# Layer two's attention sums on GpSimd and in one set of products, its steps at two places, and layer one's reciprocal last

## What is computed

```
# layer one, for each batch: softmax over the 256 keys m, then the values
attn = softmax(einsum('bnd,bdm->bnm', q, k), axis=2)
x = einsum('bcm,bnm->bcn', v, attn) + x
# layer two: 16 heads of 16, keys from the context (128, masked) and from x itself (128)
q = latents @ q_w + q_b
kv = concatenate([context, latents]) @ kv_w + kv_b
attn = softmax(where(mask, einsum(q, k) / 16, -inf))
attn_out = einsum('bhkn,bnhd->bkhd', attn, v)
attn_out = attn_out @ out_w + out_b + residual
out = gelu(rmsnorm(attn_out) @ w1 + b1) @ w2 + b2 + residual
```

## Time and profile before

| | us |
|---|---|
| runs | 2052.34, 2045.2, 2050.21 |
| median | 2050.21 |
| the profiled execution | 2044.37 |
| its span | 2042.6 |
| PE busy in it | 1849.2 (91%) |
| DVE, ACT, POOL busy | 1151.9, 973.4, 771.2 |
| mean granted clock of PE | 0.979 |
| layer one, from the start to about | 79 |
| layer two's loop, to about | 350 |

### The profile page before, as it was taken

How to read it: one execution, slowest core, us unless ns; L and a number is a source line. 1 busy time by engine, 2 the same in 40 slices (tenths; PEclk the granted TensorE clock), 3 DMA queues, 4 the chain that set the end, 5 groups by cost and what they waited for, 6 DMA issues and landing times.

```text
span 2042.6 us, 38530 instructions
## 1 busy us (share of the span) xinstructions
PE 1849.2 (91%) x15569; PEld 1566.9 (77%) x15569; DVE 1151.9 (56%) x2106; ACT 973.4 (48%) x2551; POOL 771.2 (38%) x819
## 2 busy tenths in 40 slices
PE   6788887898999999999999999999998788888798
PEld 4566665787888888888888888888877666666587
DVE  3444555445555555566665555556544677776743
ACT  4344444333444444444444444444444576675733
POOL 3322232402433435254353433425231476675500
PEclk9999999999999999999999999999999899998999
DMA  3000001101322223132231322222120000000000
GB/s 113 11 7 2 7 2 43 50 1 16 70 45 58 58 47 65 34 67 43 42 63 37 68 46 54 57 48 53 38 90 1 12 2 2 7 2 6 2 21 21
DMA packets 163201, 71.98 MB, mean 35 GB/s; under 512 B 136512, under 2 KB 154576, under 8 KB 163024
## 3 DMA queue, kind: packets, MB, share of 16 engines
q1 hardware_dynamic: 150672, 50.64, 12.6%
q10 hardware_dynamic: 12352, 18.88, 3.0%
HBM read 33.84 MB, written 2.10 MB: 18 GB/s over the span
## 4 chain that ended last, share of the span: by engine, by line
PE 75%; DVE 10%; ACT 9%; issue 3%; POOL 2%; DMA 1%; SPq 0%; ACTq 0%; DVEq 0%; POOLq 0%
PE ps_high L197 40%; PE ps_four L197 8%; PE ps_four L2667 5%; PE ps_four L2655 5%; PE ps_high L2552 2%; PE ps_high L2591 2%; ACT l_pt L1738 2%; PE ps_high L2446 1%; ACT l_sm L1783 1%; DVE l_sm L2173 1%; DVE l_sm L2183 1%; PE ps_four L2462 1%; ACT l_prob L1829 1%; PE ps_four L2467 1%; PE ps_high L2602 1%
## 5 line engine op out<-in xcount | busy, mean ns | idle before, releaser
L1839 ACT ACTIVATE l_ao<-ps_four,columns 128x512 fp32r<-128x512 f32 x128 | 88.0, 687 | 388.2 <-PE ps_four L2667 377.6
L1626 POOL TENSOR_TENSOR l_prob<-l_prob,l_mx 128x516 f32<-128x516 f32 x128 | 134.2, 1049 | 310.1 <-DVE l_mx L2214 310.1
L1829 ACT ACTIVATE l_prob<-ps_four,l_mx 128x129 f32<-128x129 f32 x512 | 181.8, 368 | 123.0 <-DVE l_mx L2207 122.8
L197 PE MATMUL ps_high<-l_hT,l_wq 128*128 128x512 f32 x768 | 210.8, 410 | 2.1 <-DVE l_hT L2096 2.1
L197 PEld LDWEIGHTS ps_high<-l_wo,l_ao 128*128 128x128 f32 x1536 | 198.0, 190 | 10.6 <-issue 0.7
L197 PE MATMUL ps_high<-l_wo,l_ao 128*128 128x256 f32 x1536 | 202.7, 281 | 0.0
L197 PE MATMUL ps_high<-l_wv,ctxT 128*128 128x512 f32 x768 | 200.3, 396 | 1.4 <-ACT l_qT L1810 1.4
L197 PE MATMUL ps_high<-ctxT,l_wk 128*128 128x512 f32 x768 | 198.5, 394 | 0.0
L1592 POOL TENSOR_TENSOR l_sm<-l_sm,l_mask 128x1024 f32<-128x1024 f32 x64 | 158.8, 2504 | 38.0 <-DVE l_sm L2173 38.0
L2220 DVE COPY l_planes<-l_prob 128x1024 uint16<-128x1024 uint16 x128 | 88.8, 694 | 149.0 <-POOL l_prob L1626 149.0
L197 PEld LDWEIGHTS ps_high<-ctxT,l_wk 128*128 128x128 f32 x768 | 144.8, 189 | 33.7 <-DVE l_V L2195 0.4
(11 more groups left out here) (295 smaller groups left out, 3791.5 us busy)
## 6 DMA issues: line engine op xcount, KB each, us to landing
l_staging<-in_L_xattn_wv ACTq DMA_DIRECT2D x8, 512.0 KB, 4.2
...
l_planesT<-l_planes SPq DMA_TRANSPOSE x128, 3.1
```

The costliest lines, as they stand in the source:

```text
L197: ins = e.matmul(out, a, b, start=start and i == 0, stop=stop and i == 2, skip_group_check=not check)
L1626: e.tensor_tensor(pr[:, :, 0:S + 1], pr[:, :, 0:S + 1], mx[:, 3, :].unsqueeze(2).to_broadcast([P, GB, S + 1]), ALU.mult).then_inc(sem("poo ...
L1829: ins = e.activation(pr.t[:, b, 0:S + 1], banks[b // 2].t[:, (b % 2) * (S + 2):(b % 2) * (S + 2) + S + 1], ACT.Exp, bias=mx[:, 1, b:b + 1] ...
L1839: e.activation(ao.t[:, 0, :], bk.t, ACT.Identity, bias=self.cols(f"L2_xattn_bv{at + 1}")[:, hd:hd + 1]).then_inc(sem("act.l2_values"), 1)
```

## The change

- **One set of sum products.** POOL adds the exponentials of the second half into the first one's tile (new stage `l1_fold`, 128x2048, in place). It waits until PE has read that tile in `over_v(n, 0)` and until the second half's exponentials are there. The 8 sum products then stand once in a batch, in a stage `l1_sums` of their own, which waits for the fold; `l1_ao` stands behind it.
- **Places.** `l1_over(n-1, s)` stand where they stood. `sums(n-1)` stands behind the shift and the first of two new `fill_pe`, directly ahead of `probs(n, 0)`. The credit is now given once a step (L1_STEPS). `fill` gives at most one advance, at two places; `fill_pe`, at two places, gives one or two and stops early at a stage with PE products. The `fill` ahead of `maxima(n, 1)` is gone.
- **Layer one.** The reciprocal and the product with it become a stage `l0_norm`, emitted last in a step.

```diff
-L1_RATE, L1_SLACK = (0.85, 1.0, 1.0, 1.0), 1
+L1_STEPS, L1_SLACK = (3.6, 4.25, 4.25, 4.25), 1
...
-            pl.free("mx", b, by=("pool.l0_scores", b))
+
+        def normalise(b):
+            pl.emit("l0_norm", b)
+            pl.free("mx", b, by=("pool.l0_norm", b))
...
-            for off, f in ((0, project), (1, softmax), (3, out), (2, values)):
+            for off, f in ((0, project), (1, softmax), (3, out), (2, values), (1, normalise)):
...
             if s == 1:
-                pl.slot(rec, "rec", n)
...
+                pl.emit("l1_fold", n)
+
+        def sums(n):
+            g, b = n // GB, n % GB
+            pl.slot(rec, "rec", n)
+            if b == 0:
+                pl.slot(ao, "ao", ("l1", g))
+            pl.emit("l1_sums", n)
+            pl.emit("l1_ao", n)
...
-            while ("l1_over", g * GB + GB - 1, 1) not in pl.place:
+            while ("l1_sums", g * GB + GB - 1) not in pl.place:
...
-        def fill(n, share=1.0):
+        def fill():
             nonlocal due
-            due += share * L1_RATE[min(n, B - 1) // GB]
-            while due >= 0.999:
+            if due >= 1.0:
                 due -= 1.0
                 next(rest, None)
+
+        def fill_pe():
+
+            nonlocal due
+            for _ in range(2):
+                at = len(pl.order)
+                due -= 1.0
+                next(rest, None)
+                if due < 0.0 or any(stage in ("l1_xT", "cols", "rows2", "out32", "norm_tr") for stage, _ in pl.order[at:]):
+                    return
...
         for n in range(B + 1):
+            due += L1_STEPS[min(n, B - 1) // GB]
...
-            fill(n, 0.25)
             if n < B:
                 maxima(n, 1)
...
-            fill(n)
+            fill()
             if n > 0:
                 over_v(n - 1, 1)
-            fill(n)
+            fill()
             if n < B:
                 run(shifted(n))
...
-            fill(n)
+            fill_pe()
+            if n > 0:
+                sums(n - 1)
             if n < B:
                 probs(n, 0)
             self.evac = "dve"
-            fill(n)
+            fill_pe()
             self.evac = "act"
...
+        def l1_fold(n):
+
+            pt = [use["pt", n, s].t for s in range(2)]
+            q.wait_ge(sem("pe.l1_over"), n + 1)
+            q.wait_ge(*pl.event(("empty", "four", n, "prob", 1)))
+            e.tensor_tensor(pt[0][:], pt[0][:], pt[1][:], ALU.add).then_inc(sem("pool.l1_fold"), 1)
...
+        def l1_sums(n):
+            pt, bk = use["pt", n, 0].t, use["over", n]
+            q.wait_ge(sem("pool.const:o"), 3)
+            q.wait_ge(*pl.done("pool.l1_fold", n))
```

More of the change, by code:

```diff
@@ L623, in over_v @@
         def over_v(n, s):
-            g, b = n // GB, n % GB
             if s == 0:
                 pl.bank(over, "over", n)
-            pl.emit("l1_over", n, s, v_done=ready[g])
+            pl.emit("l1_over", n, s, v_done=ready[n // GB])
             if s == 1:
-                pl.slot(rec, "rec", n)
-                if b == 0:
-                    pl.slot(ao, "ao", ("l1", g))
-                pl.emit("l1_ao", n)
-                pl.free("over", n)
-                pl.free("rec", n, by=("pool.l1_ao", n))
-                for s in range(2):
-                    pl.free("pt", n, s, by=("full", "over", n))
-                    if b == GB - 1:
-                        pl.free("vv", ("l1", g), s, by=("full", "over", n))
+                pl.emit("l1_fold", n)
[6 more added lines that the diff above has]
+            pl.emit("l1_ao", n)
+            pl.free("over", n)
+            pl.free("rec", n, by=("pool.l1_ao", n))
+            for s in range(2):
+                pl.free("pt", n, s, by=("full", "over", n))
+                if b == GB - 1:
+                    pl.free("vv", ("l1", g), s, by=("full", "over", n))
         def end(g):
@@ L1494, in l1_heads, with l0_norm @@
             ins.then_inc(sem("pool.l1_heads"), 1)
-        def l0_scores(b):
+        def l0_norm(b):
             pr, mx = use["prob", b].t, use["mx", b].t
-            q.wait_ge(*pl.done("dve.l0_scores:r", b))
+            q.wait_ge(*pl.done("dve.l0_norm", b))
             e.tensor_tensor(pr[:], pr[:], mx[:, 2, :].unsqueeze(2).to_broadcast([P, 2, D]), ALU.mult).then_inc(
-                sem("pool.l0_scores"), 1)
+                sem("pool.l0_norm"), 1)
         def w_pool(name, c0):
@@ L1963, in l0_scores, with l0_norm @@
                 sem("dve.l0_scores:m"), 1)
+        def l0_norm(b):
+            mx = use["mx", b]
             q.wait_ge(*pl.event(("empty", "l0_scores", b)))
-            e.reciprocal(mx.t[:, 2, :], mx.t[:, 1, :]).then_inc(sem("dve.l0_scores:r"), 1)
+            e.reciprocal(mx.t[:, 2, :], mx.t[:, 1, :]).then_inc(sem("dve.l0_norm"), 1)
         def l0_values(b):
@@ L2294, in vector_program @@
         stages = dict(const=const, l2_bws=l2_bws, l2_pbs=l2_pbs, l1_const=l1_const, rows2=rows2, l1_max=l1_max, l1_shift=l1_shift,
-                      out32=out32, norm_tr=norm_tr, cols=cols, l0_loads=l0_loads, l0_project=l0_project, l0_scores=l0_scores, l0_values=l0_values, l0_out=l0_out, w_dve=w_dve,
+                      out32=out32, norm_tr=norm_tr, cols=cols, l0_loads=l0_loads, l0_project=l0_project, l0_scores=l0_scores, l0_norm=l0_norm, l0_values=l0_values, l0_out=l0_out, w_dve=w_dve,
                       l1_xT=l1_xT, l1_key_mask=l1_key_mask, norm_stats=norm_stats, norm_var=norm_var,
@@ L2371, in l0_values @@
             pr = use["prob", b].t
-            q.wait_ge(*pl.done("pool.l0_scores", b))
+            q.wait_ge(*pl.done("pool.l0_norm", b))
             bk = fill("l0_tr", b)
@@ L2456, in l1_over @@
             q.wait_ge(*pl.event(("empty", "four", n, "prob", s)))
-            q.wait_ge(sem("pool.const:o"), 3)
             bk = fill("over", n) if s == 0 else use["over", n]
@@ L2461, in l1_over @@
                     for r in range(4):
-                        e.matmul(bk.t[32 * r:32 * r + 32, S * j:S * j + S], vv[:, b, i, j * P + 32 * r:j * P + 32 * r + 32],
-                                 pt[:, r, (2 * j + i) * S:(2 * j + i + 1) * S], start=(j, i, s) == (0, 0, 0),
-                                 stop=i == 1 and s == 1, tile_position=(0, 32 * r), skip_group_check=True)
+                        ins = e.matmul(bk.t[32 * r:32 * r + 32, S * j:S * j + S], vv[:, b, i, j * P + 32 * r:j * P + 32 * r + 32],
+                                       pt[:, r, (2 * j + i) * S:(2 * j + i + 1) * S], start=(j, i, s) == (0, 0, 0),
+                                       stop=i == 1 and s == 1, tile_position=(0, 32 * r), skip_group_check=True)
+            if s == 0:
+                ins.then_inc(sem("pe.l1_over"), 1)
+        def l1_sums(n):
+            pt, bk = use["pt", n, 0].t, use["over", n]
+            q.wait_ge(sem("pool.const:o"), 3)
+            q.wait_ge(*pl.done("pool.l1_fold", n))
             for i in range(2):
@@ L2468, in l1_over @@
                                    pt[:, r, :].rearrange("p (j i t) -> p i j t", j=2, i=2)[:, i], start=False,
-                                   stop=i == 1 and s == 1, tile_position=(0, 32 * r), skip_group_check=True)
-            if s == 1:
-                ins.then_inc(bk.slot.full, 1)
+                                   stop=i == 1, tile_position=(0, 32 * r), skip_group_check=True)
+            ins.then_inc(bk.slot.full, 1)
         def out32(t, h):
@@ L2716, in tensor_program @@
                       l1_shift=l1_shift, l1_probs=l1_probs, l1_over=l1_over,
-                      out32=out32, up3=up3, down3=down3, rows2=lambda p, h: rows(p, h, "rows2"),
+                      l1_sums=l1_sums, out32=out32, up3=up3, down3=down3, rows2=lambda p, h: rows(p, h, "rows2"),
                       l0_project=l0_project, l0_qk=l0_qk, l0_group_scores=l0_group_scores, l0_values=l0_values, l0_out=l0_out,
```

2 lines of the change are left out of this document (1 added, 1 removed).

## The result

The changed kernel takes **2068.47 us** (median of four runs, 2064.42 to 2073.07) against 2049.75 for the kernel before (four runs beside it): ratio 1.0105, 95% interval 1.0087 to 1.0123. It is slower. The forecast was 2063, in a range of 2040 to 2078, with 0.61 on slower.

The account below looks back on a forecast made before the run. PE bounds the kernel, except light steps, a chain through ACT, ps_high and DVE. Layer two -4.8+5.0+5.0+11.6=+16.8, layer one -4.0, together +12.8: 2057.2 us from the profiled 2044.4, 2063 against the median; range 2040 to 2078.

Parts of the forecast that it names:

- Light A: Layer two, a stretch from probs(n-1,1) to probs(n,0) not filled with projections: now bound by GpSimd, 8.88 becomes 9.05 us.
- B(8): Layer two, from probs(8,0) to probs(8,1): 6.45 us, +1.7, with a projection and an output product in it.
- A(10): Layer two, from probs(9,1) to probs(10,0): PE's own time, 11.45 us, 1.1 less than before.
- The held operation: Between probs(8,1) and probs(9,0), norm_var's tiny DVE operations stand until the fold ends: 3.5 us more, bounds 0 and 4.6.
- Rival 1: Layer two: norm_var's tiny operations are not held, or slip in ahead of the fold; 2053.7 us, chance 0.16.
- The last group: Layer two, from probs(12,0) to probs(15,1): 44.5 us becomes 53.7, +9.2.
- The first group: Layer two, from probs(0,1) to probs(4,0): 59.7 us becomes 53.9; with 1.0 for a third projection ahead, -4.8.
- Layer one: Evictions fill DVE's 1.09 us wait ahead of each reciprocal in layer one: -4 us, bounds 0 and -14.
- ScalarE's ring: Layer one, from a maximum through exponentials, two copies and DVE's subtraction to the next maximum: limit of 2.86 to 2.9 us.
- The clock: Third rival: PE's idle time in layer two brings the 1.2 GHz level, +8 to +15 us more, 2074; chance 0.16.
- Moved steps: Layer two: fill() and fill_pe() put two value projections and both output products later, 1.5 and 1.83 us each, PE's own.
- Sum products: Layer two: 256 records go, at most 17.2 us, 15.5 with overlap, counting in full only where PE ends last.

Follow-up runs that it names:

- e12_four_tiny: The changed kernel with norm_var's two tiny operations written as eight of 128x1, each with one tensor operand: 2055.48 us, ratio 1.0038 to the kernel before.
- e2_places: The kernel before with only the new credit, fill() and fill_pe(); no fold, sum products twice, layer one as before: 2044.45 us, ratio 0.9982.
- e1_norm: The kernel before with only layer one's reciprocal and product put last in a step: 2041.47 us, ratio 0.9976.
- e3_fold: The kernel before with the fold and one late set of sum products, the old fill and layer one as before: 2069.33 us, ratio 1.0112.
- e8_nofold: The changed kernel without the fold, both halves' sum products late, behind the shift: 2053.02 us, ratio 1.0030 to the kernel before.
- e10_both: The kernel before with the edits of e1_norm and e2_places together, no fold, no late sums: 2035.35 us, ratio 0.9940.
- e9_late_end: e2_places with a group's end also waiting until the step passes the place of the late sums, the sums unmoved: 2041.50 us, ratio 0.9968 to the kernel before.
- e11_mixed: e10_both with fold and late sums only for batches 1, 4, 5, 8, 9, and norm_var and norm_rstd behind the shift: 2036.33 us, ratio 0.9943 to the kernel before.

## Why the prediction was right, and where not

It said 2063 and +12.8; the runs say +18.7. The time came out nearer than the parts, since two misses partly cancel: from probs(0,1) to the MLP's second products the sum had +15.8 and the two profiled executions show +24.3; up to probs(0,1) it had -3.0 and they show -7.1. That is luck. By its steps:

- **The fold**, taken as 4.6: 4.54 in the mean. The figure of the Trainium skill's "GPSIMD Engine Reference", section 3.1, 4.497, agrees within 0.04. **Light A**, 9.05: 9.03 to 9.13 in A(4), A(7), A(11) and A(14). **l1_y0**, 10.85: 10.67 and 10.66 in A(8) and A(12); A(3) took 11.53, with its sums and probs at the lower clock. **B(8)** 6.45: 6.52. **A(10)** 11.45: 11.48. PE waits for the fold in 7 places, not 8 to 10; in A(7) and A(11) the norm's transposes lie in the wait.
- **The held operation**, 3.5 us: the mechanism was right, and it is shown by three kernels. It costs 2.9 on the path, by the shift's start (T+16.90, and T+13.98 in e12_four_tiny). What the sum left out is the clock behind it: A(9) was to be 20.4 and took 21.65, and it is 4.75 shorter in e12_four_tiny. The reason given, two SBUF operands, was half of it. Rival 1 (not held) is out; it was priced at 9.3 (12.8 less 3.5), and the change and e12_four_tiny differ by 10.4 in loop and tail and by 13.0 in the medians.
- **The last group**, +9.2: +12.3. A(13) took 19.55, not 17.2: the tiny operations did not get ahead of the fold. **The end** came to 10.82 for 11.0, and then 1.3 more at the lower clock (6.59 for the 18 records).
- **The first group**: 53.9 by the sum, 55.65 measured, of which A(3) and B(3) are 1.6, at the lower clock. The third projection, put at 1.0 ahead of probs(0,1), cost 0.5 there (e2_places).
- **Layer one**, -4.0: -5 to -5.9 alone (e1_norm). ScalarE's ring was taken as the limit, 2.86 to 2.9, and the period is 2.65, near the other ring that the prediction named and put aside, GpSimd's multiply and the transposes, 2.6. Which of the two sets it was not tried.
- **The clock** was made a rival with 0.16 instead of a term. It is a part of the largest stalls here: 1.8 in A(9), and more at the end and in A(3). The forecast should have carried it as a term for A(5), A(9), A(13) and the end, where its own sum had PE idle; the length of the wait alone does not tell it, as the 2.77 in A(9) of e3_fold show, with the clock full behind them.

The step that was wrong in kind is **Moved steps**. It laid the projections and output products in B(8) and A(9) to `fill()` and its places. With the places alone they stay where they were and the kernel gains (e2_places); they move with the late sums (e3_fold, e8_nofold). The sizes were right since the order was read off row by row, but the account was not, and with it the advice would have been wrong: undoing the places alone leaves most of the loss (e3_fold is as slow, without layer one's part), and undoing the fold and the late sums turns it into a gain (e10_both). e9_late_end parts it further: the output products move with the late end of a group and cost nothing by that; that the projections move with the late release of vv is read from the code.

**Sum products** was the other one. A(10) was called PE's own, so that a set which leaves it counts in full. It does take the 11.48 of the sum, but with the places alone and both sets still in it, it is as short (11.52 in e2_places). In A(2), A(6) and A(10) one of the two sets stands in a wait for exponentials and is free, though these steps are long; in A(5) and A(9) none is (e11_mixed).

What the parts cost, from the profiled executions, loop and tail together: places -4.3 (e2_places against before), late sums +12.8 (e8_nofold against e2_places), the fold +15.8 (the change against e8_nofold), of which the held operation is 10.1 of loop; and layer one -5.9. That is +18.4; the change's own execution shows +17.2 there, 1.2 less as its layer one ended 1.2 earlier than that of e1_norm. These prices hold for this order of adding. In the other order the fold and the late sums cost 18.9 together without the places (e3_fold against before), and the places, added last, cost 5.4 (the change against e3_fold) where alone they gain 4.3. Each kernel has one profiled execution, and the tail alone differs by up to 2.5 among the kernels with no fold, with the clock there.
